# P V with V as weights, softmax division before the transposes, and other moves in a six-layer local-attention kernel

## The reference, cut to what matters

```python
q, k, v = split(shift_tokens(x) @ Wqkv)
q = rope(l2norm(q) * q_scale);  k = rope(l2norm(k) * k_scale)
sim = einsum('bhwie,bhwje->bhwij', bq, bk2) * 8.0
sim = where(mask, -big, sim)
out = einsum('bhwij,bhwje->bhwie', softmax(sim, -1), bv2)
x = x + out @ Wo
xn = layernorm(shift_tokens(x)) * g + bln
a, gate = split(xn @ W1 + b1)
x = x + (a * gelu(gate)) @ W2 + b2
```

## Time and profile before

| | us |
|---|---|
| median of 3 runs (lowest, highest) | 1942.52 (1942.41, 1943.18) |
| the profiled execution: time | 1940.85 |
| the profiled execution: span | 1939.1 |
| busy: PE, DVE, ACT, POOL | 1742.4, 1436.7, 1142.3, 791.5 |

### The profile page before, as it was taken

How to read it: one execution, slowest core, us unless ns; L and a number is a source line. 1 busy time by engine, 2 the same in 40 slices (tenths; PEclk the granted TensorE clock), 3 DMA queues, 4 the chain that set the end, 5 groups by cost and what they waited for, 6 DMA issues and landing times.

```text
span 1939.1 us, 80741 instructions
## 1 busy us (share of the span) xinstructions
PE 1742.4 (90%) x35952; PEld 1405.9 (73%) x35952; DVE 1436.7 (74%) x2083; ACT 1142.3 (59%) x2065; POOL 791.5 (41%) x612
## 2 busy tenths in 40 slices
PE   6568999999899998999988999998998999999996
PEld 5247777777777777777777777777777777777775
DVE  6757768867877876887786688777778768868863
ACT  2035666666656665666665666666566666656653
POOL 1024434544443453443363344355434444534430
PEclk9679999999999999999999999999999999999998
DMA  3067565566556556646546664656665556555551
GB/s 99 1 148 167 132 143 131 121 145 163 124 136 142 121 126 174 146 113 140 135 118 160 143 145 111 139 142 153 142 146 122 127 140 142 125 139 137 116 126 40
DMA packets 98316, 252.93 MB, mean 130 GB/s; under 512 B 29872, under 2 KB 36144, under 8 KB 97200
## 3 DMA queue, kind: packets, MB, share of 16 engines
q1 hardware_dynamic: 97968, 247.76, 54.0%
HBM read 44.23 MB, written 2.10 MB: 24 GB/s over the span
## 4 chain that ended last, share of the span: by engine, by line
PE 60%; DVE 22%; POOL 6%; issue 4%; ACT 4%; DMA 2%; SPq 2%; POOLq 0%; DVEq 0%
PE ps L356 53%; PE ps L534 6%; DVE UV L729 5%; DVE mx L796 4%; POOL E L1111 4%; DVE E L790 4%; DVE zl L841 4%; ACT E L874 2%; SPq L317 1%; POOL Qtb L1101 1%; DMA rope<-in_c_rope 1%; DVE R L758 1%; ACT zr L874 1%; DVE sq L710 1%; PE ps L498 0%
## 5 line engine op out<-in xcount | busy, mean ns | idle before, releaser
L729 DVE SCALAR_TENSOR_TENSOR UV<-ps,veca,rope 128x512 f32<-128x512 f32 x768 | 523.4, 744 | 74.8 <-PE ps L356 59.5
L1101 POOL TENSOR_TENSOR Kt<-UV 128x512 f32<-128x512 f32 x192 | 242.5, 1284 | 587.4 <-DVE UV L729 587.4
L874 ACT ACTIVATE sq<-ps 128x512 f32<-128x512 f32 (+1 forms) x400 | 232.8, 582 | 274.9 <-PE ps L356 206.7
L1101 POOL TENSOR_TENSOR Qtb<-UV 128x512 f32<-128x512 f32 x192 | 241.7, 1281 | 161.8 <-DVE UV L729 161.8
L1111 POOL TENSOR_TENSOR E<-E,mx 128x1024 f32<-128x1024 f32 x96 | 182.9, 1905 | 304.1 <-DVE mx L796 296.2
L356 PE MATMUL ps<-xh,wh 128*128 128x256 f32 x768 | 238.6, 311 | 5.4 <-ACT sq L874 4.1
L356 PE MATMUL ps<-xl,wh 128*128 128x256 f32 x768 | 218.3, 284 | 3.0 <-issue 2.8
L356 PE MATMUL ps<-xh,wl 128*128 128x256 f32 x768 | 218.6, 285 | 0.4 <-issue 0.4
L356 PE MATMUL ps<-Kb,Qtb 64*32 64x64 f32 (+1 forms) x12288 | 186.5, 222 | 26.3 <-issue 25.9
L874 ACT ACTIVATE OT<-ps 128x512 f32<-128x512 f32 x192 | 104.2, 595 | 170.7 <-PE ps L534 170.2
L356 PEld LDWEIGHTS ps<-Kb,Qtb 64*32 64x32 f32 x12288 | 156.6, 106 | 52.4 <-issue 51.7
(11 more groups left out here) (132 smaller groups left out, 3746.6 us busy)
## 6 DMA issues: line engine op xcount, KB each, us to landing
V<-Vs SPq DMA_DIRECT2D x672, 128.0 KB
Kb<-Kt SPq DMA_DIRECT2D x384, 128.0 KB
Qtb<-Qtb SPq DMA_DIRECT2D x384, 128.0 KB, 2.4
rope<-in_c_rope SPq DMA_DIRECT2D x48, 512.0 KB
raw<-in_Wqkv SPq DMA_DIRECT2D x6, 1536.0 KB, 7.0
V<-Vs SPq DMA_DIRECT2D x96, 64.0 KB
V<-V SPq DMA_DIRECT2D x96, 64.0 KB, 2.0
wo<-in_Wo SPq DMA_DIRECT2D x6, 512.0 KB
```

The costliest lines, as they stand in the source:

```text
L729: e.scalar_tensor_tensor(UV[:, p % 2, slot, :].rearrange("p (i t) -> p i t", i=2), ps[:, half, :].rearrange("p (i t) -> p i t", i=2), veca ...
L874: return e.activation(out, in_, f, **kw)
L1101: e.tensor_tensor(dst, u, v, op).then_inc(s["rot_done"], 1)
```

## The change

- P V swaps its operands: V is the weight (64 columns), PT streams (32 columns), in tiles of 64 rows and 64 columns; the result has the value dimension on partitions, as the output projection wants it. On, `b_div` and `b_ot` go; Wo is permuted on the host to the new order.
- The division moves ahead of the transposes: `b_nrm` (POOL) multiplies all of E by `ri`.
- Two output tiles: OT has one for each c.
- PT goes through one PSUM bank (4) in four parts; the output projection, mu and var get bank 5; bank 7 is the FFN's.
- `a_norm` sums the squares of both pairs p of a side together, in 16 records.
- The mask is written by 8 matmuls of 32 rows and 32 columns, with tile positions (32g, 32w), g = w + r mod 4.
- `c_zh` adds the bias in an op of its own, `c_zl` becomes a plain subtraction on POOL.
- A new order, `SCHEDULE`.

```diff
-NORM, FF = 6, 7
-
-
-SCHEDULE = """b_lnq b_rcq a_rot0 a_vs0 a_vs1 a_sqy0 a_sqx0 b_sub0 a_v0 b_rq c_wo a_v1 a_xs+1 b_rqt a_rl c_xs a_x0 a_sqy1
-    b_sub1 a_y0 c_xb b_s0 a_mx0 a_my0 a_mx1 c_zsq a_my1 a_x1 a_y1 c_mu b_scale0 c_zn a_sqx1 b_s1 c_rs c_var
-    a_norm0 a_halo a_norm1 w_h1 b_max0 b_s2 a_rck b_s3 c_zl b_scale1 b_max1 a_mx2 a_x2 c_zh a_rot1 w_l1 w_h0
-    a_xh+1 a_rot2 a_y2 a_lnk a_rh b_pt0 b_exp0 c_h0 b_att0 a_my2 b_sum0 a_sqy2 a_sp0 b_pto0 a_kn0 c_hm0 a_sqx2
-    b_pt1 a_sp1 b_att1 b_exp1 c_gelu0 c_h1 a_kn1 w_l0 b_pto1 a_norm2 a_x3 a_rot3 c_gelu1 a_y3 a_xl+1 b_att2 a_sqy3
-    b_div0 a_sqx3 c_wl c_h2 c_hm1 a_mx3 b_ot0 c_gelu2 b_oto0 a_norm3 c_down w_l2 b_att3 a_my3 w_h2 b_wo b_ot1
-    c_hm2 b_sum1 c_fin c_wh b_div1 b_oto1 b_xb""".split()
+PTB, WO, NORM, FF = 4, 5, 6, 7
+
+
+SCHEDULE = """a_vs0 a_v0 a_vs1 b_lnq a_sqy0 a_sqx0 b_rcq a_v1 a_mx0 a_rot0 a_x0 a_my0 b_sub0 b_rq w_h1 b_scale0 a_sqy1
+    b_max0 c_xs b_exp0 a_mx1 a_rot1 a_y0 c_xb b_nrm0 c_zsq a_sqx1 a_halo a_xs+1 a_my1 c_rs b_sum0 b_s0 b_scale1
+    a_lnk b_rqt b_s1 a_sqy2 a_x1 b_pto0 b_sub1 c_zh a_rh a_y1 c_wo c_zl b_s2 c_mu b_s3 c_var a_norm0 a_x2 b_pto1
+    a_rl a_rck a_y2 b_pt0 b_exp1 a_rot2 a_sqx2 b_max1 b_oto0 c_zn a_mx2 a_my2 b_sum1 c_gelu0 b_pt1 b_att0 b_nrm1
+    b_att1 c_h0 w_l0 a_sp0 a_rot3 a_kn0 w_h0 a_xh+1 a_sp1 b_wo a_kn1 a_xl+1 a_x3 a_sqy3 b_pto2 a_y3 b_pt2 c_hm0
+    c_h1 a_mx3 a_my3 w_l1 b_att2 c_hm1 c_gelu1 b_xb a_sqx3 b_pt3 c_h2 b_pto3 c_hm2 a_norm1 c_gelu2 b_att3 c_wh
+    c_wl w_h2 c_fin c_down w_l2 b_oto1""".split()
...
-    mask = np.where(np.stack([first, seen], 1), 0.0, NEG)
+    mask = np.where(np.stack([first, seen, np.roll(first, W, 0)], 1), 0.0, NEG)
...
-        On = sb("On", [P, HP, 2, DH])
-        OT = sb("OT", [P, HP, P])
+        OT = sb("OT", [P, C, HP, P])
...
-        mask = sb("mask", [P, 2, KEYS], BF16)
+        mask = sb("mask", [P, 3, KEYS], BF16)
...
-            def a_norm(m, p):
-
-                e.wait_ge(s["sq_done"], m * 8 + 2 * p + 2)
-                if p == 2:
+            def a_norm(m, side):
+
+                e.wait_ge(s["sq_done"], m * 8 + 4 * side + 4)
+                if side:
                     e.wait_ge(s["rc_done"], m * 2 + 1)
-                elif p == 0 and m:
+                elif m:
                     e.wait_ge(s["rq_done"], m)
                 for half in range(2):
-                    for i in range(2):
-                        q = 2 * (p % 2) + i
-                        ins = mm(ps[q * W:(q + 1) * W, NORM, p // 2 * T:(p // 2 + 1) * T], ind[:, :],
-                                 sq[:, p % 2, half, i * T:(i + 1) * T], half == 0, half == 1, tile_position=(0, q * W))
+                    for q in range(HQ):
+                        ins = mm(ps[q * W:(q + 1) * W, NORM, side * T:(side + 1) * T], ind[:, :],
+                                 sq[:, q // 2, half, q % 2 * T:(q % 2 + 1) * T], half == 0, half == 1,
+                                 tile_position=(0, q * W))
...
-                        e.wait_ge(s["on_done"], n * C)
+                        e.wait_ge(s["ots_done"], n * 4)
                     for r in range(2):
                         if i == 0 and r == 1:
                             e.wait_ge(s["k_in"], n * 128 + 128)
-                        mm(ps[:, 2 + r, :].rearrange("p (j k) -> p j k", j=HP), identb[:, :],
-                           mask[:, chosen:chosen + 1, :].broadcast_to([P, HP, KEYS]), True, False, skip_group_check=True)
+                        for w in range(NW):
+                            g = (w + r) % NW
+                            rows, v = slice(g * W, (g + 1) * W), chosen if chosen else 2 * r
+                            mm(ps[w * W:(w + 1) * W, 2 + r, :].rearrange("p (j k) -> p j k", j=HP), identb[rows, rows],
+                               mask[rows, v:v + 1, :].broadcast_to([W, HP, KEYS]), True, False, skip_group_check=True,
+                               tile_position=(g * W, w * W))
...
-            def transposed(src, done, v2=0):
-                for h in range(HP):
-                    if h == HQ and v2:
-                        e.wait_ge(s["v2_in"], v2)
-                    ins = e.transpose(ps[:, 4 + h // 4, (h % 4) * P:(h % 4 + 1) * P], src[:, h, :, :], ident[:, :])
-                    if h % 4 == 3:
-                        ins.then_inc(s[done], 1)
-
-            def b_pt(n, c):
-                e.wait_ge(s["p_done"], n * C + c + 1)
-                if c == 1:
-                    e.wait_ge(s["pts_done"], n * 4 + 2)
-                elif n:
-                    e.wait_ge(s["ots_done"], n * 4)
-                transposed(E[:, c], "pt_done", n * 256 + 256 if c == 0 else 0)
+            def b_pt(n, i):
+                c = i // 2
+                if i % 2 == 0:
+                    e.wait_ge(s["pn_done"], n * C + c + 1)
+                if n or i:
+                    e.wait_ge(s["pts_done"], n * 4 + i)
+                for h in range(HQ):
+                    if i == 1 and h == HQ - 1:
+                        e.wait_ge(s["v2_in"], n * 256 + 256)
+                    ins = e.transpose(ps[:, PTB, h * P:(h + 1) * P], E[:, c, i % 2 * HQ + h, :, :], ident[:, :])
+                ins.then_inc(s["pt_done"], 1)
...
-                    e.wait_ge(s["on_done"], n * C + c)
+                    e.wait_ge(s["ots_done"], n * 4 + 2)
                 if i % 2 == 0:
                     mm(ps[:, 2, 0:1], identb[:, :], identb[:, 0:1])
-                    e.wait_ge(s["pts_done"], n * 4 + 2 * c + 2)
-                for h in heads:
-                    for r in range(2):
-                        for w in range(NW):
+                e.wait_ge(s["pts_done"], n * 4 + i + 1)
+                for h in heads[::2]:
+                    for w in range(NW):
+                        for r, h in ((0, h), (1, h + 1), (0, h + 1), (1, h)):
                             rows = slice(r * DH, (r + 1) * DH)
-                            ins = mm(ps[w * W:(w + 1) * W, 2 + r, h * DH:(h + 1) * DH], PT[rows, h, w * W:(w + 1) * W],
-                                     V2[rows, n % 2, C * w + c, h * DH:(h + 1) * DH], tile_position=(r * DH, w * W))
+                            ins = mm(ps[h % 2 * DH:(h % 2 + 1) * DH, 2 + r, h // 2 * P + w * W:h // 2 * P + (w + 1) * W],
+                                     V2[rows, n % 2, C * w + c, h * DH:(h + 1) * DH], PT[rows, h, w * W:(w + 1) * W],
+                                     tile_position=(r * DH, h % 2 * DH))
...
-            def b_ot(n, c):
-                e.wait_ge(s["on_done"], n * C + c + 1)
-                if c == 0:
-                    e.wait_ge(s["pts_done"], n * 4 + 4)
-                else:
-                    e.wait_ge(s["ots_done"], n * 4 + 2)
-                transposed(On[:, :, :, :], "ot_done")
-
             def out_proj(n, c):
 
                 if c == 0 and n % G == 0:
                     e.wait_ge(s["wo_in"], n // G * 16 + 16)
-                if c == 0:
-                    e.wait_ge(s["xa_done"], G + n)
-                else:
+                if c:
                     e.wait_ge(s["xb_done"], n * C + 1)
+                elif n:
+                    e.wait_ge(s["zn_done"], n)
                 e.wait_ge(s["ots_done"], n * 4 + 2 * c + 2)
                 for h in range(HP):
-                    ins = mm(ps[:, FF, 0:P], wo[:, h, :], OT[:, h, :], h == 0, h == HP - 1)
+                    ins = mm(ps[:, WO, 0:P], wo[:, h, :], OT[:, c, h, :], h == 0, h == HP - 1)
...
                     e.wait_ge(s["zl_done"], j + 1)
+                    e.wait_ge(s["xa_done"], G + j)
...
-            def b_div(n, c):
-                e.wait_ge(s["ri_done"], n * C + c + 1)
-                e.wait_ge(s["o_done"], n * C + c + 1)
-                if n or c:
-                    e.wait_ge(s["ot_done"], n * 4 + 2 * c)
-                e.tensor_tensor(On[:, :, :, :].rearrange("p j r k -> p r j k"),
-                                ps[:, 2:4, :].rearrange("p r (j k) -> p r j k", k=DH),
-                                ri[:, c].rearrange("p j r -> p r j").unsqueeze(3).broadcast_to([P, 2, HP, DH]),
-                                ALU.mult).then_inc(s["on_done"], 1)
...
-            def c_zl(j, _):
-                e.wait_ge(s["zh_done"], j + 1)
-                e.scalar_tensor_tensor(zl[:, :], zs[:, :], vecc[:, j // G % 2, LB:LB + 1], zh[:, :], ALU.add,
-                                       ALU.subtract).then_inc(s["zl_done"], 1)
...
-            def b_pto(n, c):
-                for i in range(2):
-                    e.wait_ge(s["pt_done"], n * 4 + 2 * c + i + 1)
-                    if i == 0 and (c or n):
-                        e.wait_ge(s["o_done"], n * C + c)
-                    act(PT[:, 4 * i:4 * i + 4, :], ps[:, 4 + i, :]).then_inc(s["pts_done"], 1)
+            def b_pto(n, i):
+                e.wait_ge(s["pt_done"], n * 4 + i + 1)
+                if i % 2 == 0 and (i or n):
+                    e.wait_ge(s["o_done"], n * C + i // 2)
```

(35 more changed lines are left out.)

29 lines of the change are left out of this document (14 added, 15 removed).

## The result

The change makes the kernel faster: 1860.63 us (median of 4 runs, 1851.59 to 1866.85) against 1942.47, a ratio of 0.957 [0.954, 0.961]. Forecast were 1865. The profiled execution took 1851.59 us, 9 under its median, so sums against it come out a little low.

The account below looks back on a forecast made before the run. PE's work was taken as the bound: 32.6 us of work plus 2.55 of waits gave 35.2 us a period, 1.65 less than 36.85, times 47 = 78 us, so 1865 us; range 1760 to 1950.

Parts of the forecast that it names:

- PE is the bound: TensorE is busy 34.56 of 36.85 us per period; a microsecond removed per period is worth 47 us unless a wait eats it.
- Transposes of On: The two groups of 8 transposes of On on PE disappear, taking 1.75 us off each period.
- Squares: Square sums on PE: the Q side goes from two lone groups to one of 16 records, 0.90 us less per period.
- Mask: Mask matmuls before the scores, twice a period: 0.17 us less each, 0.35 in all; bounds -0.55 and +2.7.
- P V: With V as weight, a quarter goes from 0.79 to 1.0 us, +0.8 a period; bounds 0 and +3.2.
- zl: Subtraction moved from VectorE (1.93 us mean) to POOL, expected near 0.9 there, with its 1.5 us of waiting gone.
- Regular waits: PE's waits forecast from the new order of each queue: together 2.55 us a period, against 2.3 before.
- b_pt1: Follows b_pt0 directly in a shared PSUM bank, so PE waits through the drain and ScalarE's copy: 0.9 us.
- b_pt0: First transposes of E, waiting for the scaled E through VectorE and POOL, the longest new chain: 0.4 us.
- the rival in which the waits stay small: P V keeps 0.8 a quarter and few waits remain: 33.1 us a period, 1766 us in total; chance 0.23.
- the difference of 0.35 us is layer changes and stray stalls, which I leave as they are: Gap between the mean period, 37.2 us, and an undisturbed one, 36.85, assumed unchanged by the change.
- Hidden, barely: Queries' ring, last Q projection through POOL's rotation and SP's transfers to the scores: slack falls from 3.9 to 0.7 us, no wait.

## Why the prediction was right, point by point

The time was 4 us from the forecast. The mean period's 32.57 busy and 2.55 idle look like the forecast's 32.6 and 2.55, but those were for an undisturbed period, and like for like the sum came out by two errors that cancel: 33.50 (32.25 busy, 1.25 idle) for 35.2, 80 us too dear over 47 periods, and an excess of 1.63 us for 0.35, 60 too cheap. Another 8 came in ahead of and behind the steady stretch, 199 us long where it was 191, and 9 are the profiled execution's distance to its median, of which the forecast had 1.7.

- **PE is the bound, and work taken off it counts in full:** the squares alone took 52.8 us of work and 45.6 of time.
- **Transposes of On,** -1.75: gone, and no other group took their place.
- **Squares,** -0.90: 16 records in 1.00 us, one group fewer. 52.8 / 48 = 1.1 with shorter entries around. The 1.08 of the sum is a row's own length; from its start to the next group's it was 1122.35 - 1121.19 = 1.16.
- **Mask,** -0.35 in all: 0.55 became 0.33 twice, -0.44. The step was right in the trace and shows nothing between the medians, which I had not foreseen.
- **P V,** 1.0 a quarter: 1.07 and 1.22 in the two quarters that stand alone, 2.11 in the two together, so 4.4 a period and +1.2 for +0.8, between the bounds. The term was sized somewhat low, and it stayed that small because of the order over four tiles, which the prediction had only as overlap seen before.
- **zl,** near 0.9 on POOL: 0.73. VectorE went from 28.20 to 23.77 where 25.1 was forecast: the sum took off one division of 1.22, and there were two in a period (96 in 48 steps in the earlier trace rows); with both it gives 23.8. POOL went to 21.18 (20.3), ScalarE to 23.59 (23.6).
- **Regular waits.** b_pt1: 0.74 (0.9). c_mu: 0.43 (0.5). a_v1: no idle PE, but its first matmul starts 0.46 after the one before it, where the others have 0.23: 0.23 (0.25). b_pt0 and b_att1: nothing, where I had 0.4 and 0.5; the run with a_y2 moved shows that b_pt0's chain is hidden by 0.1 to 0.2. Together 1.25 idle for 2.55: the undisturbed period is near the 33.1 of the rival in which the waits stay small.
- **The step that failed** is "the difference of 0.35 us is layer changes and stray stalls, which I leave as they are". It became 1.63. Of this growth of 1.28 us a period, 60 in all, the waits name about 35: 16.5 for the queries and 49.1 - 31.1 = 18 more at issue (31.1 within the steady window before). Another 0.28 a period, 13 us, is busy time above that of the undisturbed period (0.32 for 0.04 before). Such periods show the lower granted clock, 0.96 for 1.00 in the disturbed window above. The rest is small idle times with no name.
- **"Hidden, barely"** was the right place for the wrong reason. I gave 0.7 us of slack by a chain from a_y3 through rotation and eight issues. The chain that binds in 16 of the 18 steps that wait starts at a_kn1 and has 16 issues in it, eight of them the keys', some of which take two to four times the usual 0.59 us. It costs 16.5 us where I had nothing, and the experiment that moves half of the queries' DMAs away gains 24.

So the work was forecast by its reasons, and the waits by luck: regular ones 61 us too dear (1.3 x 47), irregular ones left as they were.
